# Third and fourth unit's maxima products set between and behind the halves of the second MLP product

## The reference

```python
m = silu(cond) @ w_ada + b_ada                      # nine shifts, scales and gates
h = _ln(x) * (1 + sc_msa) + sh_msa
x = x + g_msa * self_attn(h)      # rolled by 64, windows of 128 tokens, 16 heads of 16
h = _ln(x) * (1 + sc_mca) + sh_mca
scores = q @ k.T / 4              # against 64 context rows
top_s, top_i = top_k(scores, 16)  # per token and head
x = x + g_mca * (softmax(top_s) @ v[top_i] @ w_co + b_co)
h = _ln(x) * (1 + sc_mlp) + sh_mlp
u = h @ w_m1 + b_m1               # 256 -> 2048
x = x + g_mlp * (silu(u[:, :1024]) * u[:, 1024:] @ w_m2 + b_m2)
# second layer: adaptive layer norm on x, 16-head attention over the 64 context rows
x = x + softmax(q3 @ k1.T / 4) @ v1 @ Wp + bp
```

## Time and profile before

| | us |
|---|---|
| median of 3 runs (1036.87 to 1038.7) | 1036.92 |
| the profiled execution | 1036.82 |
| its span, first to last instruction | 1034.7 |
| TensorE matmul busy | 899.1 |
| VectorE busy | 757.4 |
| ScalarE busy | 475.9 |
| GpSimd busy | 218.4 |

### The profile page before, as it was taken

The page is one execution under the profiler, slowest core; times in us unless marked ns, Lnnn a source line. Parts: engine busy times, 40 slices in busy tenths (PEclk is TensorE's granted clock), DMA queues, the critical chain, the costliest instruction groups (busy, mean ns, idle before and its releaser), DMA issues.

```text
span 1034.7 us, 22090 instructions
## 1 busy us (share of the span) xinstructions
PE 899.1 (87%) x8088; PEld 651.1 (63%) x8088; DVE 757.4 (73%) x3953; ACT 475.9 (46%) x792; POOL 218.4 (21%) x162
## 2 busy tenths in 40 slices
PE   5977654998999989998999999998999898767975
PEld 3754542686668756785668665875778666644763
DVE  2647876898579976998589867997599858875322
ACT  3336313634564365625563456526462554315313
POOL 1015411412040222301041305020140403120010
PEclk9998686999999999999999999999999998889989
DMA  8250010000100102000100111000100110000000
GB/s 322 100 169 11 2 42 0 18 2 2 36 23 1 53 3 78 11 2 2 41 17 1 53 34 46 11 2 2 57 2 8 47 31 1 2 1 1 21 1 21
DMA packets 29051, 32.96 MB, mean 32 GB/s; under 512 B 4320, under 2 KB 26000, under 8 KB 28688
## 3 DMA queue, kind: packets, MB, share of 16 engines
q1 hardware_dynamic: 28944, 31.55, 9.3%
HBM read 25.19 MB, written 6.36 MB: 30 GB/s over the span
## 4 chain that ended last, share of the span: by engine, by line
PE 62%; DVE 24%; ACT 8%; issue 4%; DMA 1%; POOL 1%; SPq 1%; ACTq 0%; DVEq 0%; POOLq 0%
PE bank L1312 57%; DVE left L1062 7%; DVE negm L1025 5%; DVE top L1060 4%; PE bank L1479 2%; DVE negm L1087 2%; PE bank L1330 2%; ACT arena L816 2%; ACT hT L705 2%; DVE x L999 1%; DVE stats L961 1%; DVE arena L1054 1%; DMA w_m<-in_w_ada 1%; DVE arena L1079 1%; ACT rden_self L750 1%
## 5 line engine op out<-in xcount | busy, mean ns | idle before, releaser
L630 POOL TENSOR_TENSOR eS<-arena,top 128x1024 f32<-128x1024 f32 x32 | 62.0, 1936 | 278.9 <-DVE top L1060 278.9
L1312 PE MATMUL bank<-w_m,arena 128*128 128x256 f32 x512 | 115.3, 387 | 6.1 <-issue 6.1
L1312 PEld LDWEIGHTS bank<-w_m,arena 128*128 128x128 f32 x512 | 98.6, 194 | 21.3 <-issue 6.9
L1062 DVE MATCH_REPLACE8 left<-top,left 128x64 f32<-128x64 f32 x512 | 99.9, 208 | 0.0
L1062 DVE MATCH_REPLACE8 left<-top,arena 128x64 f32<-128x64 f32 x512 | 99.8, 208 | 0.0
L601 POOL TENSOR_SCALAR veps<-mv 128x4 f32<-128x4 f32 (+1 forms) x33 | 8.1, 246 | 427.7 <-DVE mv L968 427.7
L759 ACT ACTIVATE arena<-bank 128x512 f32<-128x512 f32 x128 | 66.1, 602 | 57.5 <-PE bank L1312 57.5
L805 ACT ACTIVATE rden<-bank,chan 128x512 f32<-128x512 f32 x64 | 44.1, 689 | 102.7 <-PE bank L1312 76.8
L1312 PE MATMUL bank<-qr,w_m 128*128 128x512 f32 x256 | 82.2, 402 | 3.9 <-ACT qr L715 3.2
L1025 DVE TENSOR_REDUCE negm<-bank 128x4 f32<-128x512 f32 x128 | 78.8, 681 | 3.9 <-PE bank L1312 3.0
L1312 PE MATMUL bank<-qr,m_low 128*128 128x512 f32 x256 | 80.4, 396 | 0.0
(11 more groups left out here) (133 smaller groups left out, 1837.1 us busy)
## 6 DMA issues: line engine op xcount, KB each, us to landing
w_m<-in_w_m SPq DMA_DIRECT2D x4, 1024.0 KB, 5.7
xin<-in_x SPq DMA_DIRECT2D x4, 512.0 KB, 3.9
arena<-in_w_m SPq DMA_DIRECT2D x1, 2048.0 KB, 12.9
out<-x SPq DMA_DIRECT2D x4, 512.0 KB, 2.9
arena<-in_w_ada SPq DMA_DIRECT2D x1, 1536.0 KB, 11.3
gate<-gate_rows SPq DMA_DIRECT2D x12, 128.0 KB, 3.7
gated_bias<-gate_rows SPq DMA_DIRECT2D x12, 128.0 KB, 3.8
xin<-in_x SPq DMA_DIRECT2D x4, 384.0 KB, 3.1
```

The lines of the kernel that those rows point to most:

```text
L630: nc.gpsimd.tensor_tensor(eS[:], S[:, t, :].rearrange("p (h n) -> p h n", h=H), top[:, :, 0:1].to_broadcast([P, H, LC]), ALU.subtract).the ...
L1062: i = nc.vector.match_replace(left[:, h, :], eight, scores, REPLACED)
L1312: return nc.tensor.matmul(dst, lhsT, rhs, start=start, stop=stop)
```

## The change

The amount of work is the same; its order changes on TensorE, VectorE and ScalarE in `full(a)`, and with it the rotation of banks in `bank_order`. On TensorE the third unit's maxima products stand between the halves of the second MLP product, the fourth unit's behind them, and windows 0 and 1 then follow one another; the transposes of layer 4 stand ahead of the first window's values. On VectorE the maxima of units 2 and 3 stand around the second half's residual, ahead of top-k steps 2 and 3 of the third unit; the division of window 0 stands ahead of step 4, and step 1 of the fourth unit behind the division of window 1. On ScalarE two pairs of neighbours change places.

```diff
-    def project(layer, n):
-        for u in range(2):
+    def project(layer, n, halves=(0, 1)):
+        for u in halves:
             yield ("y", layer, n, u)
...
         for w in range(2):
             yield from by_row_group("A", a, w)
-        yield from project(3, b)
+        for u in range(2):
+            yield from project(3, b, (u,))
+            yield from by_row_group("A", a, 2 + u)
         yield from window(a, 0)
-        yield from by_row_group("A", a, 2)
         yield from window(a, 1)
-        yield from by_row_group("A", a, 3)
+        yield from by_chunk("T", 4, b)
         yield ("PV", a, 0)
-        yield from by_chunk("T", 4, b)
         yield from window(a, 2)
...
                 window(a, 0)
                 window(a, 1)
+                modulated(4, b)
                 self_denominator(a, 0)
-                modulated(4, b)
                 window(a, 2)
                 last_query(b)
+                self_denominator(a, 1)
                 topk_exp(c, 3)
-                self_denominator(a, 1)
                 window(a, 3)
...
                 topk(c, 2, (0, 1))
                 residual_moments(3, b, (0,))
+                window_max(a, 2)
+                residual_moments(3, b, (1,))
+                window_max(a, 3)
+                normalise(4, b, (3, b))
                 topk(c, 2, (2, 3))
-                residual_moments(3, b, (1,))
-                window_max(a, 2)
-                normalise(4, b, (3, b))
-                window_max(a, 3)
+                window_divide(a, 0)
                 topk(c, 2, (4,))
-                window_divide(a, 0)
-                topk(c, 3, (0, 1))
+                topk(c, 3, (0,))
                 window_divide(a, 1)
+                topk(c, 3, (1,))
                 last_max(b)
...
-                project(3, b)
+                for u in range(2):
+                    project(3, b, (u,))
+                    scores_for_max(a, 2 + u)
                 window(a, 0)
-                scores_for_max(a, 2)
                 window(a, 1)
-                scores_for_max(a, 3)
-                window_values(a, 0)
                 if a == 2:
                     pe.wait_ge(s_wlast, 32)
                 transposed(4, b)
+                window_values(a, 0)
                 window(a, 2)
```

## The result

The changed kernel takes 1076.64 us in the median of 4 runs (1068.04 to 1077.88), the kernel before beside it 1036.89 (1031.29 to 1038.7): a ratio of 1.0375, 95% interval 1.0308 to 1.0442. Slower by 40 us. The forecast was 1073.

What follows compares the result with a forecast made beforehand. It took TensorE (87% busy) as the bound for most of each block, alternating with VectorE and ScalarE in the reordered stretch. 1036.8 + 25.8 (six blocks, 4.3 late each) + 10.5 (clock falls) = 1073 us, range 1054 to 1080.

Steps and rivals of the forecast that it cites:

- The back of the stretch: VectorE's new order: the moved top-k step (3.2 us) queues ahead of `last_max`, which starts 4.3 late including earlier delay.
- The front: TensorE's new order and bank rotation up to window 2: window 2 0.9 us late, its second part 1.1 late.
- The clock: TensorE's clock falls behind the new 4.0 us gap ahead of window 3: 2.1 a fall, five of six blocks, 10.5.
- rival 3: TensorE's stalls of 1.4, 1.0 and 1.1 ahead of the gap also bring the clock down: over 1080 us; chance 0.07.
- Rival 1: Delay ahead of window 3 without clock falls, or with one or two: 1062.6 up to 1066 us; chance 0.22.
- The sum: Whole kernel: 1036.8 + 25.8 for six delayed blocks + 10.5 for clock falls = 1073 us.
- Rival 4: Three TensorE waits vanish and VectorE's pause of 2.25 absorbs the moved step: faster, 1026 us; chance 0.04.
- Rival 2: VectorE's waits turn out shorter, hiding part of the delay: 2 to 3 a block, 1049 to 1055 us; chance 0.08.

Runs made afterwards that it cites:

- the version with the step put back: Changed kernel with step 1 of the fourth unit's top-k again ahead of window 1's division on VectorE: 1045.09 us, ratio 1.0069 to the kernel before.
- the step alone: Kernel before with only step 1 of the fourth unit's top-k moved behind window 1's division, ahead of `last_max`: 1066.55 us, ratio 1.0253.
- the half-step version: Changed kernel with step 1 of the fourth unit's top-k cut in two, eight heads on each side of window 1's division: 1061.57 us, ratio 1.0237.

## Why the prediction was right

**The back of the stretch: right.** Worked out 3.7 of idle time ahead of the second division, measured 3.70. Worked out 3.2 for the step, measured 3.10 as the difference of two clean blocks (116.42 and 113.32), with the step itself at 3.11. The gap ahead of window 3: 4.0 worked out, 3.84 measured. The step that counts is not a long one, nor is it new work. VectorE does all its steps in order, the one moved had filled an idle time ahead of a division that waits for ScalarE, and behind the division everything is on the path. The chain of before shows this without an experiment: the division and `last_max` follow each other in it.

**The front: right in kind and nearly in size.** 1.1 worked out, 0.94 measured. The two waits on banks were put at 1.4 and 0.35 and came out at 1.29 and 0.47; the idle time of VectorE ahead of the second half's residual at 2.4, measured 2.74. The wait for the copy of window 1's transposed maxima was put too high, 1.0 worked out and 0.40 measured; TensorE's timeline of the version with the step put back has it at the full clock:

```profile
466.30 0.67 PE L1312 MATMUL bank<-mTs,head_rows 32*128 32x128 f32 x16 [0.40 <-ACT mTs L755]
```

The Trainium skill's rule on rotating groups (Perfetto Trace Analysis, "Matmuls") points at the waits of two windows in a row. The whole front costs 0.94 a block, the small part; how much of it is due to the two windows, to ScalarE's new order or to the fourth unit's maxima no run here tells apart.

**The clock: right in the sum, the chance was set too low.** 2.1 a fall was worked out from matmuls at the lower level elsewhere in the trace of before, and 2.1 is the measured mean; that the two are equal is partly luck, since single blocks gave 1.05 to 2.78 and one of the five holds a second fall. I took five falls in six; there were six behind the gap and, by the windows, two more at the front, which was rival 3's mechanism (0.07) without its time. Rival 1, delay without falls, had 0.22. The traces don't bear it out: behind 3.84 the clock fell in twelve blocks of twelve (the changed kernel and the step alone), and even behind 2.29 in six of six. One of the four executions of the changed kernel took only 1068.04; it has no trace, so what it was spared stays open. The gaps of 3.9 and more were the wrong yardstick. They were also miscounted: six of them begin at the full level in the trace of before, not four (ahead of 102.63, 136.05, 168.68, 897.12, 919.50 and 1003.18), and all six have a fall. And before already held nearer rows: a gap of 2.29 ahead of 71.39 and one of 2.61 ahead of 865.63, both with a fall, and the one block of 113.43, whose clock fell in this same stretch though no gap in it is over 0.9. The Trainium skill (TensorE: Matmul & The Clock Gate, "Part 1: The HAM clock gate") has the gate on its own count, which doesn't restart with the kernel. The traces agree so far as the stretches at the lower level vary in length from block to block behind the same gap, with blocks of 116.25 to 117.77 in the half-step version.

**The sum.** Blocks: 6 x (0.94 + 3.10 + 2.1) = 36.8 against 36.3 on record. The profiled execution is 41.1 longer. What is left, about 4, lies in the fill ahead of the first block (2.4), where nothing was changed and the clock fell at other places than before, and in the sixth block and the drain. Over the nine traces here the first MLP start lies anywhere from 189.75 to 197.19, with the same program ahead of it. How much of that is due to the change and how much is the spread between executions (before itself ran from 1031.3 to 1043.4 over the sessions) stays open.

**The rivals.** Rival 4, faster, was to be decided by whether the second division is ready before 474.6 on the time scale of before; it was ready at 481.9 (496.82 less 14.88). Rival 2, part of the delay hidden: the clean block grew by 3.10 for a step of 3.11, so nothing of it was hidden.

## What to carry to other kernels

When a step is moved past a wait on an in-order engine, ask what stands behind the wait: idle time ahead of a wait is free room for off-path work, and the first place behind it belongs to whatever the critical engine waits for. Work out the rotation of the banks again when results change places; a group that waits for all its banks waits for the last reader of any of them. And price a new gap on TensorE with the clock behind it: here a gap of 3.84 cost another 2.1 in the mean, one of 2.29 by estimate 1.4 to 2.9.

## What the runs showed of the hardware

Keeping TensorE busy with matmuls whose results nobody uses made a program faster: seven in each gap of 3.84 kept the granted clock at full behind the gap, in all six blocks, and took the ratio from 1.0375 to 1.0242.

And the length of a gap alone doesn't tell whether the clock falls. Behind the gap of 2.29 in the half-step version it fell in six blocks of six, and in the kernel before it fell in one block behind gaps of 0.9 and less. In the fill all nine traces have a gap of 2.29 ahead of the same transposes. Behind it the clock fell in eight of them and stayed at full in the changed kernel's. The kernel before and the changed one:

```profile
71.39 1.64 PE L1330 MATMUL bank<-ident,xh 128*128 128x128 f32 x8 [2.29 <-DVE xh L973]
```

```profile
73.00:77.00 4.00, 3.15 (x5) 1.52 (x5) 1.25 (x4) 1.45 (x2) 0.00 (x0) 0.53 0.96 300
```

```profile
70.11 1.64 PE L1331 MATMUL bank<-ident,xh 128*128 128x128 f32 x8 [2.29 <-DVE xh L973]
```

```profile
73.00:77.00 4.00, 3.28 (x8) 1.14 (x6) 1.79 (x8) 1.54 (x3) 0.18 (x1) 1.00 0.82 240
```

The changed kernel's clock had fallen some 14 us earlier instead, behind a gap of 2.08 (ahead of 54.85); the same gap, 2.08 or 2.09 long, left it at full in the eight others.
